# An attention and feed-forward kernel: VectorE copies transposed tiles out ahead of the bias and minimum of the row four ahead

## The chip, the cores and the metric

The kernel runs on one core of a Trainium2 chip. The time is device microseconds of one execution: 1320.96 us, the median of three runs (1320.94 to 1322.1).

## The reference

The input x is 4 batches of 1024 tokens with 128 channels, all float32. Attention has 16 heads of 64 channels; heads are worked two at a time, and such two are called a pair here.

```python
q, k, v = jnp.einsum('bsx,xMnd->Mbnsd', x, qkv)
a = jnp.einsum('bnsd,bntd->bnst', q, k) * 64 ** (-0.5)
cum = jnp.cumsum(rpe_bias, axis=-1)                    # 16 heads x 256 distances
rel = jnp.arange(s)[:, None] - jnp.arange(s)[None, :]
bias = jnp.where(rel >= 0, cum[:, jnp.clip(rel, 0)], -30000.0)   # causal
a = jax.nn.softmax(a + bias, axis=-1)
mix = jnp.einsum('bnst,bntd->bnsd', a, v)
x = layernorm(x + jnp.einsum('bnsd,ndx->bsx', mix, out_w))
# then token-wise: xr, xk mix each token with the one before it
r = sigmoid(xr @ W_r);  k_act = relu(xk @ W_k) ** 2
x = layernorm(x + r * (k_act @ W_v))
```

## The kernel before

**Steps and slots.** The work is 4 batches times 8 pairs of heads, 32 pair steps. A pair step has 16 rows of attention: a row is one head and one tile of 128 queries, and it is as wide as the causal keys before it, 128 x (i + 1) for tile i. `ROWS` lists them: rows 0 to 3 are head 0 with tiles 0 to 3, rows 4 to 7 head 1 with the same tiles, rows 8 to 11 head 0 with tiles 4 to 7, and rows 12 to 15 head 1 with tiles 4 to 7. A step has a slot for each row. Each engine has its own instruction stream, written out by hand in that order of slots, and they meet at counting semaphores.

**A row's way.** TensorE computes the scores into the PSUM tile `ps_rows` (`score`, line 904: q and k are each split into a high and a low part, which are stacked by DMAs). VectorE adds the table of biases and keeps the row's minimum (scores carry the opposite sign), writing to `prob` and `low` (`bias`, line 614). ScalarE takes the exponential and its sum (`exps`, line 470). VectorE takes the reciprocal of the sum (`invert`, line 621). GpSimd multiplies the row by it (`normalise`, line 421). TensorE transposes the row's 128x128 tiles into two PSUM tiles, `ps_t[0]` and `ps_t[1]` in turn (`transpose`, line 918). VectorE or ScalarE copies them to `pt` (`evacuate`, lines 631 and 481): the string `EVACUATOR` names for each of a step's 24 groups of up to four tiles which engine does it. VectorE has those of slots 0, 2, 5, 6, 8 (the first group), 9 (both), 10 (the first), 11 (the first) and 14 (the first). Last, TensorE multiplies `pt` with v into `ps_o` (`mix`, line 934).

**Leads and buffers.** In slot s TensorE, VectorE and ScalarE handle scores, bias and exponential of row s + 4 (`LEAD`), and VectorE the reciprocal of row s + 3; transposes and copies are of row s. `ps_rows` holds four narrow rows or two wide ones: scores of row r wait until VectorE has read the row whose place they take, which is `rows_since(r)` rows earlier: 4 for rows 3 to 7, 3 for rows 1, 2 and 8, 2 for rows 9 to 15 and for row 0. `prob` has eight buffers. A group of transposes waits for the copy of the group two before it.

**The next pair's projections.** In slots 2, 3, 5 and 7 TensorE projects q and k of the next pair (line 879), in slots 10 and 14 v. ScalarE writes the high part (`q_hi`, `k_hi`, line 457) from the PSUM tile `ps_m`, VectorE the remainder (`q_lo`, `k_lo`, line 600), and SyncE's queue then stacks them by DMA. TensorE's next use of `ps_m` waits for the remainder.

**Order within a slot.** TensorE: scores of row s + 4, projection, tile work, `mix` (slots 2, 5 and 11), transposes of row s. ScalarE: high part of the projection, tile work, copies of row s, exponential of row s + 4. VectorE: bias of row s + 4, reciprocal of row s + 3, remainder of the projection, copies of row s, copy of the mixed result to `mix_sb` (slots 6 and 12), tile work. The tile work is output projection, norms and the feed-forward part of one tile of 128 tokens; it is spread over the slots of pair steps 9 to 31. The last batch's eight tiles are worked at the end.

Of the kernel before, what the change touches and what calls it, by code (L numbers as in the profile page):

```python
# [40 lines left out]
def score_at(r):  # L41


    if r < NROWS // 2:
        return BANK * (r % 4)
    width = P * (ROWS[r][1] + 1)
    return SEQ * (r % 2) + ((SEQ - width) // 2 if width - BANK < SHORTEST else 0)
# [41 lines left out]
def build(nc, x, qkv, out_w, rpe, w_r, w_k, w_v, mu_r, mu_k, out):  # L89
# [13 lines left out]
    with ExitStack() as ctx:  # L103
# [148 lines left out]
        def rows_ahead(n, more, slot):  # L252

            if slot + LEAD < NROWS:
                return [(n, slot + LEAD)]
            return [(n + 1, slot + LEAD - NROWS)] if more else []
# [319 lines left out]
        def _(dve):  # L576
# [17 lines left out]
            def project(m, c):  # L594

                dve.wait_ge(s_hi, 4 * m + c + 1)
                which, at = chunk_of(m, c)
                hi, lo, scale = ((q_hi, q_lo, SCALE), (k_hi, k_lo, 1.0))[which]
                half = slice(512 * at, 512 * at + 512)
                nc.vector.scalar_tensor_tensor(out=lo[:, half], in0=proj_bank(m, c), scalar=scale,  # L600
                                               in1=hi[:, half].bitcast(F32), op0=ALU.mult, op1=ALU.subtract)\
                    .then_inc(s_lo, 1)

            def bias(n, r):

                h, i = ROWS[r]
                width = P * (i + 1)
                if i % GROUP == 0:
                    dve.wait_ge(s_table[n % 2][h], 16 * (n // 2) + 16)

                before = (r - PSLOTS) % NROWS
                dve.wait_ge(s_tr, NBANKS * (n if before > r else n + 1) + sum(b[0] <= before for b in BANKS))
                dve.wait_ge(s_score, NROWS * n + r + 1)
                nc.vector.tensor_tensor_reduce(prob[:, r % PSLOTS, 0:width],  # L614
                                               ps_rows[:, score_at(r):score_at(r) + width],
                                               table[n % 2][:, h, SEQ - width:], 1.0, 3.0e38, ALU.add, ALU.min,
                                               low[:, r:r + 1]).then_inc(s_biased, 1)

            def invert(n, r):
                dve.wait_ge(s_exp, NROWS * n + r + 1)  # L620
                nc.vector.reciprocal(inv[:, r:r + 1], total[:, r:r + 1]).then_inc(s_inv, 1)  # L621

            def evacuate(n, k):
                r, b0, nb = BANKS[k]
                h, i = ROWS[r]
                g = i // GROUP
                dve.wait_ge(s_pv, 2 * n + g + 1)
                if n == 0 and r == 2 * GROUP:
                    dve.wait_ge(s_xt_dram, 16)
                dve.wait_ge(s_tr, NBANKS * (n + 1) + k + 1)  # L630
                nc.vector.tensor_copy(pt[h][g][:, b0:b0 + nb, P * (i % GROUP):P * (i % GROUP) + P],  # L631
                                      ps_t[k % 2][:, 0:nb * P].rearrange("p (b s) -> p b s", s=P)).then_inc(s_ev[0], 1)

            def store_mix(n, g):
                dve.wait_ge(s_pv, 2 * n + g + 3)
                dve.wait_ge(s_mix_d[g], 16 * n + 16)
                nc.vector.tensor_copy(mix_sb[g][:, :], ps_o[:, :]).then_inc(s_o, 1)  # L637
# [66 lines left out]

            def step(n, prev, tile_too, more):
                for slot in range(NROWS):
                    for row in rows_ahead(n, more, slot):
                        bias(*row)
                    for row in rows_ahead(n, more, slot - 1):
                        invert(*row)  # L710
                    if more and slot in PROJ_SLOTS[:4]:
                        project(n + 1, PROJ_SLOTS.index(slot))
                    for k in range(NBANKS):
                        if BANKS[k][0] == slot and EVACUATOR[k] == "0":
                            evacuate(n, k)
                    if prev and slot == MIX_FAR[1] + 1:
                        store_mix(n - 1, 1)
                    if slot == MIX_NEAR + 1:
                        store_mix(n, 0)
                    if tile_too:  # L720
                        tile_step(n, slot)

            drive(step)

            def add_residual(w):
# [359 lines left out]
```

## Time and profile before

| | |
|---|---|
| median of three runs | 1320.96 us |
| the profiled execution, its own time | 1322.12 us |
| its span, first to last instruction | 1320.3 us |
| mean granted TensorE clock | 0.965 |
| TensorE, matmuls | 1121.6 us busy, 85% |
| VectorE | 890.1 us busy, 67% |
| ScalarE | 745.8 us busy, 56% |
| GpSimd | 590.8 us busy, 45% |

The profile is of one execution. A busy share is an average over the whole span, a start-up and an end among it. In its views PE is TensorE, DVE is VectorE, ACT ScalarE, POOL GpSimd and SPq the DMA queue of SyncE. A row such as `PE ps_t L918 [0.77 <-DVE pt L631]` says that TensorE stood idle for 0.77 us before the transposes of line 918, and that what ended it was VectorE's copy of line 631. Names of tiles stand without their buffer numbers.

### The profile page before, as it was taken

The numbers are of one execution on the slowest core, as the hardware profiler recorded it, in microseconds if no ns is written. First come the engines' busy times: TensorE is split into PE (matmuls) and PEld (weight loads), VectorE is DVE, ScalarE is ACT, GpSimd is POOL, SyncE is SP. The second block draws the span as 40 slices with busy tenths as digits, with TensorE's granted clock in tenths as the row PEclk, the third lists the DMA queues.
The fourth block names the chain that finished last, engine by engine and source line by source line (L and its number), as shares of the span: only waits on it lengthen the run. The fifth ranks groups of instructions, "written<-read, shape, count | busy, mean of one in ns | idle before, by whom it ended". The sixth has DMA issues, their size and how long they took to land.

```text
span 1320.3 us, 21982 instructions
## 1 busy us (share of the span) xinstructions
PE 1121.6 (85%) x6909; PEld 784.3 (59%) x6909; DVE 890.1 (67%) x2505; ACT 745.8 (56%) x1857; POOL 590.8 (45%) x527
## 2 busy tenths in 40 slices
PE   4424999999999898988998989889898988998985
PEld 2313666666666666666666666656666666666664
DVE  1422666666667777777777777777777787777756
ACT  2312666666665656565566566656656565566532
POOL 1221555555554444454444454544444454444420
PEclk9666999999999999999999999999999999999987
DMA  5775555555555445566544555655555565544610
GB/s 142 167 85 143 130 131 130 130 130 131 140 130 124 116 126 134 126 150 155 127 117 117 133 124 144 150 130 118 132 126 133 128 150 142 120 119 111 205 35 19
DMA packets 104353, 168.38 MB, mean 128 GB/s; under 512 B 10656, under 2 KB 66352, under 8 KB 104240
## 3 DMA queue, kind: packets, MB, share of 16 engines
q1 hardware_dynamic: 104240, 166.98, 52.9%
q8 instruction: 58, 0.95, 0.3%
q14 instruction: 55, 0.45, 0.1%
HBM read 41.63 MB, written 24.64 MB: 50 GB/s over the span
## 4 chain that ended last, share of the span: by engine, by line
PE 61%; DVE 16%; issue 7%; DMA 6%; ACT 6%; SPq 2%; POOL 1%; DVEq 0%; ACTq 0%
PE ps_o L934 20%; PE ps_t L918 15%; PE ps_rows L904 12%; PE ps_m L879 6%; DMA bias_by_distance<-x_t 5%; DVE prob L614 4%; PE ps_m L948 3%; DVE pt L631 3%; PE ps_m L884 3%; DVE shift L681 2%; ACT pt L481 2%; DVE mix_sb L637 2%; DVE k_lo L600 1%; ACT prob L470 1%; DVE q_lo L600 1%
## 5 line engine op out<-in xcount | busy, mean ns | idle before, releaser
L421 POOL TENSOR_TENSOR prob<-prob,inv 128x128 f32<-128x128 f32 (+7 forms) x512 | 583.5, 1147 | 676.8 <-DVE inv L621 676.2
L470 ACT ACTIVATE prob<-prob,low 128x128 f32<-128x128 f32 (+7 forms) x512 | 395.3, 773 | 144.7 <-DVE low L614 140.5
L614 DVE CUSTOM_DVE_ANT_0 prob<-ps_rows,table 128x128 f32<-128x128 f32 (+7 forms) x512 | 383.2, 748 | 120.8 <-PE ps_rows L904 90.4
L904 PE MATMUL ps_rows<-stacks 128*128 128x512 f32 (+3 forms) x1536 | 403.7, 373 | 64.0 <-DMA stacks<-k_lo 40.2
L918 PE MATMUL ps_t<-ident,prob 128*128 128x128 f32 x2304 | 351.8, 280 | 101.1 <-ACT pt L481 64.1
L918 PEld LDWEIGHTS ps_t<-ident,prob 128*128 128x128 f32 x2304 | 262.6, 141 | 213.4 <-issue 123.4
L904 PEld LDWEIGHTS ps_rows<-stacks 128*128 128x128 f32 x1536 | 247.4, 192 | 82.3 <-DMA stacks<-k_lo 40.5
L631 DVE COPY pt<-ps_t 128x256 f32<-128x256 f32 (+2 forms) x320 | 178.5, 566 | 163.5 <-PE ps_t L918 162.4
L481 ACT ACTIVATE pt<-ps_t 128x128 f32<-128x128 f32 (+2 forms) x448 | 203.4, 476 | 146.8 <-PE ps_t L918 146.8
L934 PE MATMUL ps_o<-pt,v_pair 128*64 128x512 f32 (+3 forms) x1536 | 268.7, 492 | 0.0
L934 PEld LDWEIGHTS ps_o<-pt,v_pair 128*64 128x64 f32 x1536 | 101.9, 137 | 181.8 <-issue 172.3
L879 PE MATMUL ps_m<-x_cur,w_cur 128*128 128x512 f32 x250 | 131.9, 610 | 3.9 <-DVE q_lo L600 2.4
L621 DVE RECIPROCAL inv<-total 128x1 f32<-128x1 f32 x512 | 81.7, 160 | 66.0 <-ACT prob L470 64.4
L457 ACT ACTIVATE q_hi<-ps_m 128x512 fp32r<-128x512 f32 x63 | 37.2, 590 | 120.0 <-PE ps_m L879 117.5
L470 ACT ACTIVATION_READ_ACCUMULATOR prob<-prob,low 128x1 f32 x512 | 98.1, 192 | 0.0
L884 PE MATMUL ps_m<-w_cur,x_cur 128*128 128x128 f32 x504 | 66.4, 275 | 0.0
L884 PEld LDWEIGHTS ps_m<-w_cur,x_cur 128*128 128x128 f32 x504 | 65.2, 192 | 0.0
L600 DVE SCALAR_TENSOR_TENSOR q_lo<-ps_m,q_hi 128x512 fp32r<-128x512 f32 x63 | 43.6, 692 | 30.4 <-ACT q_hi L457 30.4
L491 ACT ACTIVATE lnv<-mv,eps 128x1 f32<-128x1 f32 x48 | 14.1, 294 | 80.5 <-DVE mv L683 43.6
L879 PEld LDWEIGHTS ps_m<-x_cur,w_cur 128*128 128x128 f32 x250 | 43.5, 191 | 14.9 <-issue 6.8
L462 ACT ACTIVATE v_pair<-ps_m 128x512 f32<-128x512 f32 x63 | 37.6, 596 | 25.9 <-PE ps_m L884 25.5
L948 PE MATMUL ps_m<-wo,mix_tile 128*128 128x128 f32 x384 | 47.4, 277 | 0.0
(106 smaller groups left out, 607.6 us busy)
## 6 DMA issues: line engine op xcount, KB each, us to landing
stacks<-k_hi SPq DMA_DIRECT2D x124, 256.0 KB, 4.9
stacks<-k_lo SPq DMA_DIRECT2D x124, 256.0 KB, 4.9
stacks<-q_hi SPq DMA_DIRECT2D x62, 256.0 KB, 4.5
stacks<-q_lo SPq DMA_DIRECT2D x62, 256.0 KB, 4.8
mix_transposed<-mix_sb SPq DMA_DIRECT2D x62, 256.0 KB, 2.0
table<-bias_by_distance SPq DMA_DIRECT2D x64, 192.0 KB, 2.6
mix_tile<-mix_transposed SPq DMA_DIRECT2D x24, 512.0 KB, 4.8
w_cur<-in_L_attn_qkv SPq DMA_DIRECT2D x32, 192.0 KB, 3.2
```

The source lines that it names most:

```text
L421: nc.gpsimd.tensor_tensor(row, row, inv[:, r:r + 1].broadcast_to([P, width]), ALU.mult)\
L470: nc.scalar.activation(row, row, ACT.Exp, bias=low[:, r:r + 1], scale=-1.0, accum_out=total[:, r:r + 1]).then_inc(s_exp, 1)
L481: nc.scalar.activation(pt[h][g][:, b0:b0 + nb, P * (i % GROUP):P * (i % GROUP) + P], ps_t[k % 2][:, 0:nb * P].rearrange("p (b s) -> p b s" ...
L614: nc.vector.tensor_tensor_reduce(prob[:, r % PSLOTS, 0:width], ps_rows[:, score_at(r):score_at(r) + width], table[n % 2][:, h, SEQ - width ...
L621: nc.vector.reciprocal(inv[:, r:r + 1], total[:, r:r + 1]).then_inc(s_inv, 1)
L631: nc.vector.tensor_copy(pt[h][g][:, b0:b0 + nb, P * (i % GROUP):P * (i % GROUP) + P], ps_t[k % 2][:, 0:nb * P].rearrange("p (b s) -> p b s ...
L879: ins = nc.tensor.matmul(proj_bank(m, c), w_cur[m % 2][:, which, :], x_cur[:, 512 * at:512 * at + 512], start=True, stop=True)
L884: ins = nc.tensor.matmul(proj_bank(m, c)[:, P * t:P * t + P], x_cur[:, at:at + P], w_cur[m % 2][:, 2, :], start=True, stop=True)
L904: ins = nc.tensor.matmul(ps_rows[:, at + c0:at + c1], q_st(h, n)[:, P * i:P * i + P], k_st(h, n, low_part)[:, c0:c1], start=(low_part == 0 ...
L918: ins = nc.tensor.transpose(ps_t[k % 2][:, P * b:P * b + P], prob[:, r % PSLOTS, at:at + P], ident[:, :])
L934: ins = nc.tensor.matmul(ps_o[D * h:D * h + D, c0:], v_pair[n % 2][:, j, D * h:D * h + D], pt[h][g][:, j, c0:], start=(j == 0), stop=(j == ...
L948: ins = nc.tensor.matmul(ps_m[:, 0:C], mix_tile[:, p, :], wo[:, p, :], start=(p == 0), stop=(p == PAIRS - 1))
```

## The change

VectorE's stream alone is reordered. In each slot the bias and minimum of row s + 4 and the reciprocal of row s + 3 move behind the projection's remainder and the copies of row s. They still stand ahead of the copy to `mix_sb` and of the tile work. The slots without a remainder or a copy of VectorE (1, 4, 12, 13 and 15) stay as they were.

```diff
--- before.py
+++ after.py
@@ -704,15 +704,15 @@
 
             def step(n, prev, tile_too, more):
                 for slot in range(NROWS):
-                    for row in rows_ahead(n, more, slot):
-                        bias(*row)
-                    for row in rows_ahead(n, more, slot - 1):
-                        invert(*row)
                     if more and slot in PROJ_SLOTS[:4]:
                         project(n + 1, PROJ_SLOTS.index(slot))
                     for k in range(NBANKS):
                         if BANKS[k][0] == slot and EVACUATOR[k] == "0":
                             evacuate(n, k)
+                    for row in rows_ahead(n, more, slot):
+                        bias(*row)
+                    for row in rows_ahead(n, more, slot - 1):
+                        invert(*row)
                     if prev and slot == MIX_FAR[1] + 1:
                         store_mix(n - 1, 1)
                     if slot == MIX_NEAR + 1:
```

## Rows read from the trace of the kernel before

**Rows 1.** The page, busy us of each engine (share of the span).

```profile
PE 1121.6 (85%) x6909; PEld 784.3 (59%) x6909; DVE 890.1 (67%) x2505; ACT 745.8 (56%) x1857; POOL 590.8 (45%) x527
```

**Rows 2.** Windows, 300 to 1200 us: busy us (instructions) of each engine, granted clock, DMA share.

```profile
300.00:1200.00 900.00, 815.44 (x5086) 570.29 (x5083) 667.78 (x1864) 549.79 (x1388) 436.00 (x381) 1.00 0.55 132
```

**Rows 3.** Waits, 300 to 1200 us: us in total, times, longest.

```profile
DVE pt L631 <- PE ps_t L918: 121.5, 96, 2.7
...
PE ps_t L918 <- ACT pt L481: 51.4, 47, 1.3
...
PE ps_t L918 <- DVE pt L631: 20.6, 27, 1.2
```

**Rows 4.** Timeline of TensorE, one tile step: start, us, operation, count, idle before.

```profile
710.66 0.55 PE L918 MATMUL ps_t<-ident,prob 128*128 128x128 f32 x3
...
714.14 0.95 PE L904 MATMUL ps_rows<-stacks 128*128 128x512 f32 x4
...
718.18 0.44 PE L918 MATMUL ps_t<-ident,prob 128*128 128x128 f32 x2
...
719.52 1.18 PE L904 MATMUL ps_rows<-stacks 128*128 128x512 f32 x4
...
723.01 0.96 PE L904 MATMUL ps_rows<-stacks 128*128 128x512 f32 x4
...
725.18 0.85 PE L918 MATMUL ps_t<-ident,prob 128*128 128x128 f32 x6 [0.77 <-DVE pt L631]
...
735.21 0.85 PE L918 MATMUL ps_t<-ident,prob 128*128 128x128 f32 x6 [0.96 <-ACT pt L481]
```

**Rows 5.** Timeline of VectorE, the same step.

```profile
711.31 0.56 DVE L631 COPY pt<-ps_t 128x384 f32<-128x384 f32 x1 [2.34 <-PE ps_t L918]
...
718.72 0.42 DVE L631 COPY pt<-ps_t 128x256 f32<-128x256 f32 x1 [0.63 <-PE ps_t L918]
...
724.35 0.69 DVE L631 COPY pt<-ps_t 128x512 f32<-128x512 f32 x1
...
732.43 0.69 DVE L631 COPY pt<-ps_t 128x512 f32<-128x512 f32 x1 [1.41 <-PE ps_t L918]
```

**Rows 6.** Groups by shape, 300 to 1200 us: count, busy us, mean ns, idle before.

```profile
L614 DVE CUSTOM_DVE_ANT_0 prob<-ps_rows,table 128x1024 f32<-128x1024 f32 x48 | 58.2, 1213 | 1.9 <-PE ps_rows L904 1.8
...
L614 DVE CUSTOM_DVE_ANT_0 prob<-ps_rows,table 128x896 f32<-128x896 f32 x48 | 52.1, 1086 | 10.7 <-PE ps_rows L904 10.6
...
L470 ACT ACTIVATE prob<-prob,low 128x896 f32<-128x896 f32 x48 | 50.0, 1042 | 57.6 <-DVE low L614 55.8
...
L614 DVE CUSTOM_DVE_ANT_0 prob<-ps_rows,table 128x768 f32<-128x768 f32 x48 | 45.5, 949 | 0.0
...
L614 DVE CUSTOM_DVE_ANT_0 prob<-ps_rows,table 128x512 f32<-128x512 f32 x48 | 33.1, 689 | 3.5
...
L600 DVE SCALAR_TENSOR_TENSOR q_lo<-ps_m,q_hi 128x512 fp32r<-128x512 f32 x47 | 32.5, 692 | 17.5 <-ACT q_hi L457 17.5
...
L470 ACT ACTIVATE prob<-prob,low 128x384 f32<-128x384 f32 x47 | 28.6, 608 | 0.0
...
L457 ACT ACTIVATE q_hi<-ps_m 128x512 fp32r<-128x512 f32 x47 | 27.7, 590 | 90.2 <-PE ps_m L879 90.2
...
L614 DVE CUSTOM_DVE_ANT_0 prob<-ps_rows,table 128x384 f32<-128x384 f32 x47 | 25.5, 542 | 2.3 <-PE ps_rows L904 2.3
```

**Rows 7.** Timeline of TensorE, one step without tile work.

```profile
266.77 0.55 PE L918 MATMUL ps_t<-ident,prob 128*128 128x128 f32 x3
...
269.53 0.94 PE L904 MATMUL ps_rows<-stacks 128*128 128x512 f32 x4
...
280.58 0.85 PE L918 MATMUL ps_t<-ident,prob 128*128 128x128 f32 x6 [1.21 <-DVE pt L631]
```

**Rows 8.** Timeline of ScalarE, the tile step of rows 4.

```profile
733.35 1.14 ACT L470 ACTIVATE prob<-prob,low 128x1024 f32<-128x1024 f32 x1
```

**Rows 9.** Timeline of TensorE, after slot 11 of the first step.

```profile
115.20 0.80 PE L904 MATMUL ps_rows<-stacks 128*128 128x256 f32 x2 [40.24 <-DMA stacks<-k_lo]
```

## The prediction

> **What bounds the kernel now.** I read the page's head first: of a span of 1320.3 us TensorE is busy for 85% of it, VectorE (DVE) for 67%, ScalarE (ACT) for 56% [rows 1]. The stretch from 300 to 1200 us, which the loop of pair steps fills, has TensorE busy for 815 of 900 us at granted clock 1.00, its 2.4 GHz level [rows 2]. So TensorE sets the pace, and a change elsewhere counts only where it moves one of TensorE's waits. Next the table of waits for that stretch: TensorE waits before its transposes 51.4 us for ACT's copies of transposed tiles and 20.6 us for DVE's, while DVE spends 121.5 us waiting for the transposes it is to copy [rows 3]. The last number is the one to keep in mind: on DVE the copy is an instruction that often waits for TensorE, and what stands behind it waits too. Last the timelines of a pair step, one engine at a time, to see which wait ends last in each slot [rows 4, 5, 8].
>
> **What the change moves.** Nothing is added or removed: 16 slots per pair step, and in each DVE ran bias(s+4), invert(s+3), then projection remainder and copies of slot s. Now the remainder and the copies come first. DVE copies in slots 0, 2, 5, 6, 8, 9 (two), 10, 11, 14: there the bias of row s+4, which needed only scores that TensorE computes at the slot's start, now waits for the transposes that TensorE makes at the slot's end. Three kinds of work wait for that bias: the scores two rows on, since in the wide half two rows fill the PSUM area (row 9 needs bias 7, row 11 needs bias 9, row 13 needs bias 11); ACT's exponential, and behind it in ACT's queue the next projection copy (q_hi, k_hi) and ACT's own copies of transposes; and DVE's q_lo or k_lo, which needs that q_hi or k_hi, with the following bias behind it. The last makes a ladder that crosses from DVE to ACT and back.
>
> The arithmetic: one DVE operation starts some 0.09 us before the printed end of a copy or remainder; a row minimum is readable by ACT about its printed duration after the bias's start, plus 0.03; and from DVE's last result to a matmul I take 0.14, as where the transposes at 725.18 follow the copy that ends at 724.35 + 0.69 = 725.04 [rows 4, 5].
>
> **Place A, scores of row 9 (slot 5).** The transposes of slot 2 follow a long product and end at 710.66 + 0.55 = 711.21; the copy starts at 711.31 [rows 4, 5]. Now behind it: copy 0.47, bias 6 0.54, handover 0.03, its exponential 0.61 on ACT, then q_hi 0.59 (it stood ready before), handover 0.03, q_lo 0.61, bias 7 0.69, handover 0.14 [rows 6]. 711.31 + 3.71 = 715.02, where row 9's scores started at 714.14 [rows 4]: 0.88 us. In a step without the token-wise tile work (the first nine) the copy starts 0.10 after 267.32, and 267.42 + 3.71 = 271.13 against 269.53 [rows 7]: 1.60 us.
>
> **Place B, scores of row 11 (slot 7).** The copy of slot 5 starts at 718.72 and takes 0.33 [rows 5], bias 9 takes 0.95 [rows 6], handover 0.14: 720.14 against 719.52 [rows 4], 0.62 us. It counts from the transposes of slot 5, so it adds to A.
>
> **Place C, scores of row 13 (slot 9).** From the minimum of row 9: copy of slot 6 0.47, bias 10 1.09, 0.03, exponential 10 1.04, k_hi 0.59, 0.03, k_lo 0.61, bias 11 1.21, 0.14 = 5.21. The scores of row 11 start 0.14 after that minimum, and 3.49 us lay between them and those of row 13 before (723.01 - 719.52) [rows 4, 6]. 5.21 - 0.14 - 3.49 = 1.58 us. The copy of the mixed result in slot 6 stands beside ACT's exponential and costs nothing; without that cover it would be at most 0.60.
>
> **What is gained.** The copy of slot 8 no longer stands behind bias 12, and TensorE's wait of 0.77 us for it in slot 9 goes (1.21 in the short step) [rows 4, 7]: after C it would come 0.5 us before TensorE asks. Its sum over the stretch is most of the 20.6 us of [rows 3].
>
> **Place D, transposes of slot 13.** They waited 0.96 us for an ACT copy that stands behind exponential 15 [rows 4]. That began at 733.35 behind ACT's copy of slot 11 [rows 8]. Now bias 15 stands behind DVE's copy of slot 11: 732.43 + 0.60 + 1.21 + 0.03 = 734.27 [rows 5, 6]: 0.92 us later, and all of it reaches TensorE, which waited already. The next wait of that kind (slot 14, through DVE's second normalisation and ACT's reciprocal root) hangs on the same exponential and shifts along, without a term of its own.
>
> Slots 0, 9, 10 and 14: their biases come late too, but TensorE has 16 products in slot 0 and the mixes in slots 2 and 11 before it needs them; I take 0, bounds -0.1 and 0.3 each. GpSimd's normalisation waits for DVE often and is done a slot or more ahead; 0. On SP's queue the stacking of k for the next pair waits for k_lo 3, which comes as late as C has it, and so do the scores that need it: 0; if its slack is gone, up to 1 us a step. A lies between 0 (if q_hi gets ahead) and 1.60, C between 0.3 (no ladder through ACT) and 2.2 (with the copy of the mix in it).
>
> **Sum.** A tile step: 0.88 + 0.62 + 1.58 - 0.77 + 0.92 = 3.23; a short one 1.60 + 0.62 + 1.58 - 1.21 + 0.92 = 3.51. There are 22 tile steps with a next pair and 8 short ones after the first. In the first step the delay falls into the 40.24 us for which TensorE waits for a DMA anyway [rows 9]: 0. The last has no projection, hence no ladder: 1, from B, D and the lost wait. 22 x 3.23 + 8 x 3.51 + 1 = 100 us. The profiled execution took 1322.1 us with a span of 1320.3, and the runs' median is 1321.0: 1421 us on the runs' scale.
>
> A rule that speaks for this: the Trainium skill (PSUM — Partial Sum Buffer, Engine vs sequencer instructions) has DVE's, ACT's and GpSimd's queues as strict FIFO. By it a ready bias can't pass a waiting copy, and the sum is the 100 us above; were it not so, A to D would be near nothing and the 27 us of gain (rival 1) would stand. No row before the change has a ready bias behind a waiting copy for long, so the trace leaves it to the result.
>
> **Rivals.** (1) *Slack takes it up: faster.* Rows are scored four ahead and the probabilities have eight buffers; DVE idles a third. If the bias of row s+4 were back before TensorE reaches the scores two rows on, only the gain is left: 22 x 0.77 + 8 x 1.21 = 27 us, 1294 us. It decides at B: 0.90 us lie between the end of slot 5's transposes and row 11's scores, and the way over DVE takes 1.52. Against it is that every term of B is a row. (2) *Direct waits only.* The ladders through ACT are shorter than I put them, because waits that I count as new overlap: B and D remain, less the gain: (0.77 x 22 + 0.33 x 8) = 20 us, 1341 us. For it: ACT is busy only 56% [rows 1]. (3) *Knock-on.* The late biases use up SP's slack and the stacks of the next pair arrive late, 1 us a step more: 1451 us. (4) *The clock falls.* More short waits let TensorE's granted clock drop from its 2.4 to its 1.2 GHz level. For a tenth of the 815 us in which it is busy that would be some 80 us more: 1500 us. Against it: the clock stays at 1.00 through waits of 0.77 and 0.96 us in every step [rows 2, 4]. The Trainium skill (TensorE: Matmul & The Clock Gate, A second HAM failure mode) warns of such cycling through PSUM with short idles; the trace so far does not show it.
>
> **Chances.** Forecast 0.62; rival 1 0.06; rival 2 0.16; rival 3 0.11; rival 4 0.03; 0.02 that nothing measurable happens. A difference under about 0.2% can't be told from none. Faster 0.06, same 0.03, slower 0.91. The forecast's own range is 1390 to 1440 us; to leave out no more than two in ten I take 1350 to 1450.
>
> **What would show it.** Right: bias rows directly behind copies on DVE; a new entry "TensorE scores wait for DVE's row minimum" of some 3 us a step, at rows 9, 11 and 13; "ACT exponential waits for DVE" much larger; TensorE's wait for DVE's copies near nothing; the wait in slot 13 near 1.9 us; a tile step of 41.3 us. Wrong: no wait before the scores of row 11 (B fails and with it all), or waits at B and D alone (rival 2), or scores of row 0 that wait for a stack DMA (rival 3), or a clock below 1.00 (rival 4).

## The result

The changed kernel took 1450.36 us (median of four runs, 1448.45 to 1452.84), the kernel before 1321.53 in the same set: a ratio of 1.0969, 95% interval 1.0954 to 1.0984. It is 129 us slower, where 100 were forecast. Among all runs below, two executions ran in a slower state, one of copies_only (1465.8 us, mean clock 0.901) and one of the kernel before (2828 us), and no ratio uses them.

The page of the changed kernel, busy us of each engine, and the window of 300 to 1200 us (busy us and instructions, granted clock, DMA share, GB/s), beside [rows 1, 2]:

```profile
PE 1178.6 (81%) x6909; PEld 808.7 (56%) x6909; DVE 879.4 (61%) x2505; ACT 750.2 (52%) x1857; POOL 594.2 (41%) x527
```

```profile
300.00:1200.00 900.00, 772.90 (x4566) 529.98 (x4566) 586.51 (x1669) 497.37 (x1253) 397.09 (x346) 0.98 0.49 119
```

The instructions are the same and in the same number. TensorE issued 5086 of its matmuls in this stretch before, 4566 now. Its busy sum over the whole span has grown by 57 us for the same 6909 matmuls, and the granted clock has left 1.00: some matmuls ran at the lower level. That isn't all of the 57 us: all_but_slot11 below keeps the clock at 1.00 in this stretch and has 1152.2 us, 31 more than before. The profile models the ends of matmuls, so the sum of their times is a rough measure of TensorE's work.

Its waits from 300 to 1200 us (us in total, times, longest), beside [rows 3]; the first line is of the kernel before, the others of the changed one:

```profile
ACT prob L470 <- DVE low L614: 86.6, 93, 3.0
```

```profile
ACT prob L470 <- DVE low L614: 308.1, 208, 4.5
DVE pt L631 <- PE ps_t L918: 217.1, 143, 3.5
...
PE ps_t L918 <- POOL prob L421: 42.3, 22, 1.9
...
PE ps_rows L904 <- DVE low L614: 35.3, 63, 1.3
...
PE ps_t L918 <- ACT pt L481: 23.0, 39, 1.6
...
PE ps_m L879 <- DVE y L650: 4.5, 19, 0.6
...
PE ps_t L918 <- DVE pt L631: 1.8, 7, 0.4
```

TensorE's wait for DVE's copies has gone from 20.6 to 1.8 us: the copies do come earlier. DVE spends 217 instead of 121.5 us in front of copies, and ACT's exponentials wait 308 instead of 87 us for DVE. A new line stands there: the scores wait 63 times, three times a step, for a row minimum. It sums to 35.3 us, some 1.7 us a step, where the prediction looked for some 3: the scores come nearly as late as forecast, but part of the lateness shows on other lines (TensorE waits 0.80 us for q_lo at 783.14 before it transposes x1, 0.39 before) or between other instructions. The entry "POOL prob" is slot 13's wait under another name: GpSimd's release is the last one the profile can pair with it, but row 13 had been normalised at 759.22 + 1.47 = 760.69 us, 4.6 us before the transposes began. What came last is ACT's copy, which begins at 764.53 and frees the first of its two PSUM tiles at about 765.1.

TensorE's timeline in the changed kernel, slots 13 and 14 of one tile step and 2 to 9 of the next, beside [rows 4]:

```profile
765.25 1.01 PE L918 MATMUL ps_t<-ident,prob 128*128 128x128 f32 x6 [1.92 <-POOL prob L421]
...
766.71 1.91 PE L884 MATMUL ps_m<-w_cur,x_cur 128*128 128x128 f32 x8
...
779.45 0.55 PE L918 MATMUL ps_t<-ident,prob 128*128 128x128 f32 x3
...
783.75 0.98 PE L904 MATMUL ps_rows<-stacks 128*128 128x512 f32 x4 [0.17 <-DVE low L614]
784.85 1.10 PE L879 MATMUL ps_m<-x_cur,w_cur 128*128 128x512 f32 x2
...
788.18 0.44 PE L918 MATMUL ps_t<-ident,prob 128*128 128x128 f32 x2
...
790.08 1.20 PE L904 MATMUL ps_rows<-stacks 128*128 128x512 f32 x4 [0.31 <-DVE low L614]
...
795.13 0.98 PE L904 MATMUL ps_rows<-stacks 128*128 128x512 f32 x4 [1.05 <-DVE low L614]
...
796.39 0.82 PE L918 MATMUL ps_t<-ident,prob 128*128 128x128 f32 x6
```

And DVE's and ACT's, beside [rows 5, 8]: the copy of slot 11 with bias 15 behind it, then the one of slot 5 with bias 9; and exponential 15.

```profile
761.52 0.69 DVE L631 COPY pt<-ps_t 128x512 f32<-128x512 f32 x1 [2.38 <-PE ps_t L918]
762.13 1.22 DVE L614 CUSTOM_DVE_ANT_0 prob<-ps_rows,table 128x1024 f32<-128x1024 f32 x1
...
788.73 0.42 DVE L631 COPY pt<-ps_t 128x256 f32<-128x256 f32 x1 [1.42 <-PE ps_t L918]
789.07 0.95 DVE L614 CUSTOM_DVE_ANT_0 prob<-ps_rows,table 128x768 f32<-128x768 f32 x1
```

```profile
763.39 1.15 ACT L470 ACTIVATE prob<-prob,low 128x1024 f32<-128x1024 f32 x1 [0.84 <-DVE low L614]
```

Before, bias 15 ran in the time in which DVE now stands idle for 2.38 us before slot 11's copy. Measured from the start of the long product of slot 2 to the next, a tile step went from 38.10 to 42.07 us, a step without tile work from 34.40 to 38.09. These are the usual lengths; some steps are up to 1.8 us longer, and the experiments show why.

### The profile page after: what moved, and what is told of

Read it like the earlier page. It is cut to its first block, busy times and chain, and to the rows that moved or that the text cites. A ratio compares the mean times of both kernels' runs of the same rounds, so it can differ in the third digit from the quotient of the medians.

```text
span 1451.1 us, 21982 instructions
## 1 busy us (share of the span) xinstructions
PE 1178.6 (81%) x6909; PEld 808.7 (56%) x6909; DVE 879.4 (61%) x2505; ACT 750.2 (52%) x1857; POOL 594.2 (41%) x527
## 4 chain that ended last, share of the span: by engine, by line
PE 59%; DVE 15%; issue 12%; ACT 6%; DMA 6%; SPq 1%; POOL 1%; DVEq 0%; ACTq 0%
PE ps_o L934 18%; PE ps_t L918 14%; PE ps_rows L904 13%; DVE prob L614 7%; PE ps_m L879 6%; DMA bias_by_distance<-x_t 5%; PE ps_m L948 3%; PE ps_m L884 3%; ACT prob L470 2%; DVE shift L681 2%; DVE pt L631 1%; ACT pt L481 1%; POOL prob L421 1%; ACT q_hi L457 1%; PE ps_rows L1007 1%
## 5 line engine op out<-in xcount | busy, mean ns | idle before, releaser
L904 PE MATMUL ps_rows<-stacks 128*128 128x512 f32 (+3 forms) x1536 | 412.5, 378 | 118.5 <-DVE low L614 80.0
L918 PE MATMUL ps_t<-ident,prob 128*128 128x128 f32 x2304 | 367.9, 286 | 104.2 <-POOL prob L421 60.2
L918 PEld LDWEIGHTS ps_t<-ident,prob 128*128 128x128 f32 x2304 | 273.0, 145 | 217.0 <-POOL prob L421 111.4
L904 PEld LDWEIGHTS ps_rows<-stacks 128*128 128x128 f32 x1536 | 251.2, 194 | 158.4 <-DVE low L614 80.2
L884 PE MATMUL ps_m<-w_cur,x_cur 128*128 128x128 f32 x504 | 78.6, 307 | 0.0
L884 PEld LDWEIGHTS ps_m<-w_cur,x_cur 128*128 128x128 f32 x504 | 74.0, 218 | 4.0 <-issue 4.0
L600 DVE SCALAR_TENSOR_TENSOR k_lo<-ps_m,k_hi 128x512 fp32r<-128x512 f32 x62 | 42.9, 691 | 45.8 <-ACT k_hi L457 45.8
L948 PEld LDWEIGHTS ps_m<-wo,mix_tile 128*128 128x128 f32 x384 | 46.1, 196 | 0.0
L637 DVE COPY mix_sb<-ps_o 128x512 f32<-128x512 f32 x64 | 43.6, 681 | 2.0 <-PE ps_o L934 2.0
```

The source lines that it names most:

```text
L884: ins = nc.tensor.matmul(proj_bank(m, c)[:, P * t:P * t + P], x_cur[:, at:at + P], w_cur[m % 2][:, 2, :], start=True, stop=True)
L904: ins = nc.tensor.matmul(ps_rows[:, at + c0:at + c1], q_st(h, n)[:, P * i:P * i + P], k_st(h, n, low_part)[:, c0:c1], start=(low_part == 0 ...
L918: ins = nc.tensor.transpose(ps_t[k % 2][:, P * b:P * b + P], prob[:, r % PSLOTS, at:at + P], ident[:, :])
L948: ins = nc.tensor.matmul(ps_m[:, 0:C], mix_tile[:, p, :], wo[:, p, :], start=(p == 0), stop=(p == PAIRS - 1))
```

## The experiments

All of them rearrange DVE's slot as in this diff; `EARLY` names the slots with the new order (the changed kernel has all sixteen).

```diff
+                    rows() if slot not in EARLY else None      # bias(s+4), invert(s+3)
+                    remainder()                                # project(n + 1, ...)
+                    copies()                                   # evacuate(n, k) of this slot
+                    rows() if slot in EARLY else None
```

Step lengths in us, a step without tile work and a tile step, read from TensorE's timelines as above; where some were longer, the length without a fall of the clock first:

| kernel | no tile work | tile step | median us |
|---|---|---|---|
| before | 34.40 | 38.10 | 1321.5 |
| changed | 38.09 | 42.07 | 1450.4 |
| slots2and3_alone | 35.96 | 39.32 | 1361.4 |
| slot5_alone | 34.94 | 38.63 | 1338.5 |
| slots5to8 | 35.39 | 39.40 | 1358.4 |
| slot11_alone | 35.35, 36.95 | 39.30, 40.97 | 1385.6 |
| slot11_filled | 35.35 | 39.30 | 1362.7 |
| all_but_slot11 | 37.18 | 40.88 | 1406.5 |
| changed_filled | 38.10 | 42.07 | 1442.3 |
| slot8_alone | 33.70 | 37.87 | 1310.9 |
| slot8_and_late_exp | 33.70 | 37.43 | 1301.6 |

### Place A: slots 2 and 3

```diff
+EARLY = (2, 3)
```

> The new order in slots 2 and 3 alone (place A). Theory: the scores of row 9 start 0.88 us later in a tile step and 1.6 in one without; 22 x 0.88 + 8 x 1.6 = 32 us, 1353 us. The changed kernel shows in addition 0.3 us between these scores and the next projection, because ScalarE's copy of the transposed x1 stands behind exponential 7; if that belongs to this place, 39 us, 1360 us. Rival, DVE makes it up by slot 9 where TensorE waits anyway: at most 0.77 us a step given back, 1336 us.

Measured: 1361.41 us, ratio 1.0295 (1.0280 to 1.0310), 40 us more. Steps are 1.56 us longer without tile work (1.60 forecast) and 1.22 with it (0.88 forecast). In a tile step the scores of row 9 themselves come 0.81 us late, counted from the start of slot 2's transposes (736.64 - 732.35 = 4.29 us here, 3.48 before). Another 0.33 stands right behind them: 737.75 - 736.64 = 1.11 us lie between these scores and the third projection, where 0.78 lay before (784.85 - 783.75 = 1.10 in the changed kernel). ACT's copy of the transposed x1, which frees `ps_m`, stands behind exponential 7. Nothing is made up later: the wait in slot 9 is still 0.77 us.

### Place B: slot 5

```diff
+EARLY = (5,)
```

> The new order in slot 5 alone (place B). Theory of the prediction, each place costs its own term: the scores of row 11 start 0.56 to 0.62 us later, 31 x 0.6 = 19 us, 1340 us. Rival, the terms don't add but share a cover: what sets the transposes of slot 9 before is a chain through bias 10, which moves by only 0.43 us, and the wait of 0.77 us there shrinks by the rest: 31 x 0.43 = 13 us, 1334 us.

Measured: 1338.52 us, ratio 1.0121 (1.0106 to 1.0136), 16 us more, 0.54 us a step. The time lies between the two theories' 0.43 and 0.6; the timeline decides. The rival needs the wait in slot 9 to shrink by 0.2 us, and it has not:

```profile
1082.04 0.85 PE L929 MATMUL ps_t<-ident,prob 128*128 128x128 f32 x6 [0.76 <-DVE pt L632]
```

It was 0.77 us before. All of place B reaches the end of the step.

### Places B and C and the lost wait: slots 5 to 8

```diff
+EARLY = (5, 6, 7, 8)
```

> The new order in slots 5 to 8: place B, place C and the lost wait of slot 9 together, without A and D. Theory, the places add up: the changed kernel's step is 3.97 us longer, of which A alone took 1.22 and D alone 1.20 in a tile step, so 1.55 remain; in a step without tile work 3.70 - 1.56 - 0.95 = 1.19. 23 x 1.55 + 8 x 1.19 = 45 us, 1367 us, the clock at its upper level. Rival, places share their cover (A's delay is part of C's): over 2 us a step here, 1385 us.

Measured: 1358.35 us, ratio 1.0270 (1.0248 to 1.0293). Steps grew by 0.99 and 1.30 us, so places C and slot 8 together cost 0.45 and 0.76 us; 1.58 - 1.21 = 0.37 and 1.58 - 0.77 = 0.81 were forecast. The expectation took all that A and D left for this group and was 0.2 us a step too high. The places are nearly independent: 1.56 + 0.99 + 0.95 = 3.50 of 3.69 us, and 1.22 + 1.30 + 1.20 = 3.72 of 3.97. Of the rest, some 0.2 us a tile step stand in slot 0, where the copy now delays the bias and with it the first addition of the tile work, for which the projection waits (the line "DVE y L650" above). Without tile work some 0.2 us come from slot 14: in all_but_slot11 the exponential of row 2 waits 0.39 us for its bias, which now stands behind slot 14's copy, ACT's copies of slot 15 follow that exponential, and TensorE waits for them 0.39 us before the transposes of slot 0, where it waited 0.16.

### Place D: slot 11, and the clock

```diff
+EARLY = (11,)
```

> The new order in slot 11 alone. Theory of place D: exponential 15 starts 0.92 us later and ScalarE's copies for slot 13 with it, so TensorE's wait in slot 13 is 1.9 us instead of 0.96: 31 x 0.92 = 29 us more, 1350 us, with the clock at its upper level throughout. Rival, that the long wait also brings the clock down as it stood at 0.50 in the changed kernel after it: 0.3 to 0.5 us more in each of the 23 tile steps, 1357 to 1362 us, and a granted clock below 1.00 in slots 13 and 14 of the tile steps.

Measured: 1385.61 us, ratio 1.0484 (1.0419 to 1.0549), 63 us more: twice what the place was worth by the first theory, and beyond the second too. TensorE's timeline of slots 13 to 15 in a long tile step:

```profile
728.24 0.85 PE L929 MATMUL ps_t<-ident,prob 128*128 128x128 f32 x6 [1.91 <-POOL prob L422]
...
729.28 1.82 PE L895 MATMUL ps_m<-w_cur,x_cur 128*128 128x128 f32 x8
731.91 1.73 PE L929 MATMUL ps_t<-ident,prob 128*128 128x128 f32 x7 [0.81 <-ACT pt L482]
...
734.29 1.91 PE L929 MATMUL ps_t<-ident,prob 128*128 128x128 f32 x8
```

The wait is 1.91 us, as place D said. But behind it the seven transposes take 1.73 us instead of 0.96 and the v projection 1.82 instead of 1.05: TensorE is at its 1.2 GHz level here, with a granted clock of 0.50 from 730 to 736 us. To see whether the wait is the cause, the next kernel fills it, with the scores of row 1 computed five times over instead of once:

```diff
-                    for low_part in range(2):
+                    for low_part in (0, 1) * (5 if r == 1 and n > 0 else 1):
```

> The new order in slot 11 alone, as before, and TensorE computes the scores of row 1 five times over (the same numbers, in the 0.5 us each that fall into slot 13's wait of 1.9 us): more work, in a wait. Theory, the time beyond place D's 29 us is the clock, which falls after that wait: with the wait filled to some 0.6 us it stays up, 1351 to 1357 us, faster than without the added work (1386 us). Rival, the clock is not tied to this wait, or the late exponential costs more than D says: 1386 us or above.

Measured: 1362.67 us, ratio 1.0312 (1.0271 to 1.0353). TensorE does 248 matmuls more than in slot11_alone and the kernel is 23 us faster. The same slots in its timeline:

```profile
712.45 1.43 PE L915 MATMUL ps_rows<-stacks 128*128 128x256 f32 x10
714.86 0.84 PE L929 MATMUL ps_t<-ident,prob 128*128 128x128 f32 x6 [0.97 <-POOL prob L422]
715.46 0.60 PE L915 MATMUL ps_rows<-stacks 128*128 128x384 f32 x2
715.90 1.05 PE L895 MATMUL ps_m<-w_cur,x_cur 128*128 128x128 f32 x8
718.53 0.96 PE L929 MATMUL ps_t<-ident,prob 128*128 128x128 f32 x7 [1.58 <-ACT pt L482]
```

The wait is cut to 0.97 us, the clock stays up, and all but a few steps are 35.35 or 39.30 us long. So place D by itself is 0.95 us without tile work, as forecast, and 1.20 with it. The 0.25 more in a tile step is in slot 14's wait, 1.58 us here against 1.33 in the kernel before:

```profile
738.63 0.95 PE L918 MATMUL ps_t<-ident,prob 128*128 128x128 f32 x7 [1.33 <-ACT pt L481]
```

It goes with DVE's second addition of the tile work (the last section). The time came out 6 to 12 us above the expectation; four of its tile steps were still 40.9 us long.

> The changed kernel with the old order in slot 11. Theory D: the wait in slot 13 is back at 0.96 us. If D counts 0.95 to 1.2 us a step and nothing else goes, 31 x 1.0 = 31 us less than the changed kernel, 1419 us. If the low stretches of the clock come from slot 13's wait of 1.9 us alone, they go too, and another 5 to 30 us with them, 1389 to 1414 us, with steps all of one length and a granted clock of 1.00 from 400 us on.

```diff
+EARLY = tuple(s for s in range(16) if s != 11)
```

Measured: 1406.45 us, ratio 1.0641 (1.0625 to 1.0657), 44 us less than the changed kernel, within the second theory. 8 x 0.91 + 23 x 1.19 = 35 of them are the steps of usual length; the other 9 should then be the clock's. The changed kernel with slot 13's wait filled in the same way tests that:

```diff
+EARLY = tuple(range(16))
-                    for low_part in range(2):
+                    for low_part in (0, 1) * (5 if r == 1 and n > 0 else 1):
```

> The changed kernel, with the scores of row 1 computed five times over in slot 13's wait of 1.9 us. Removing slot 11's part from the changed kernel gave 44 us, of which 8 x 0.91 + 23 x 1.19 = 35 us are the steps of full clock; theory: the remaining 9 us are the clock's, and with the wait filled they go, 1441 us, all tile steps 42.07 us long. Rival: other waits of the changed kernel, 1.05 us before the scores of row 13 the longest, keep the clock falling, 1450 us.

Measured: 1442.27 us, ratio 1.0916 (1.0893 to 1.0940), 8 us less than without the added work, and the window of 300 to 1300 us is at 1.00 again:

```profile
300.00:1300.00 1000.00, 869.88 (x5303) 597.17 (x5302) 668.65 (x1871) 554.30 (x1398) 443.15 (x386) 1.00 0.49 119
```

For comparison the changed kernel, where the clock falls after slot 13's wait for some 3 us (columns: busy us and instructions of PE, PEld, DVE, ACT, POOL, then the granted clock):

```profile
761.60:764.00 2.40, 1.69 (x14) 1.32 (x12) 2.40 (x5) 1.21 (x2) 0.49 (x1) 1.00 0.77 165
764.00:766.00 2.00, 0.75 (x7) 0.78 (x7) 1.74 (x7) 1.66 (x6) 2.00 (x2) 0.95 0.77 225
766.00:768.00 2.00, 2.00 (x11) 2.00 (x10) 1.93 (x4) 0.23 (x1) 1.04 (x1) 0.50 0.38 136
768.00:770.00 2.00, 1.69 (x11) 1.43 (x11) 0.79 (x5) 1.97 (x7) 0.40 (x1) 0.70 0.11 33
```

### Copies alone, remainder alone

```diff
-                    remainder()
                     copies()
                     rows()
+                    remainder()
```

> In all slots only the copies move ahead of bias and reciprocal; the projection's remainder stays behind them, in the order copies, bias, reciprocal, remainder. Theory: places B (0.54) and D (0.95) and the gain of slot 8 are the copies' own and stay; place C goes, because bias 11 no longer waits for k_lo, and place A shrinks from a late bias 7 to a late q_lo before the transpose of x1, up to 0.7 us in tile steps. Sum 0.8 to 1.4 us a step and the clock's part of slot 11 (30 us), 1375 to 1400 us. Rival, the copies are harmless and the remainder does it all: within 10 us of 1322.

Measured: 1442.9 us, ratio 1.0907 (1.0885 to 1.0928). Both theories fail: the copies alone cost nearly as much as the whole change. Place C did shrink: row 13's scores start 717.53 - 713.17 = 4.36 us after row 11's, against 5.05 in the changed kernel and 3.49 before (from [rows 4]). What I had missed is in slot 3, TensorE's timeline and then DVE's:

```profile
704.34 1.17 PE L889 MATMUL ps_m<-x_cur,w_cur 128*128 128x512 f32 x2 [1.39 <-DVE q_lo L601]
```

```profile
702.60 0.56 DVE L632 COPY pt<-ps_t 128x384 f32<-128x384 f32 x1 [4.61 <-PE ps_t L928]
...
703.62 0.67 DVE L601 SCALAR_TENSOR_TENSOR q_lo<-ps_m,q_hi 128x512 fp32r<-128x512 f32 x1
```

The remainder q_lo of slot 2 now stands behind that slot's copy, which waits for the transposes behind the long product, and TensorE can't project again before it. In the old order and in the changed one the remainder is ahead of that copy. The timelines are of the execution of 1465.8 us. They show the order that makes the wait; how long it is in the other executions wasn't seen, and how the 121 us divide over the places wasn't measured.

```diff
                     remainder()
-                    copies()
                     rows()
+                    copies()
```

> In all slots only the projection's remainder moves ahead of bias and reciprocal (slots 2, 3, 5 and 7), the copies stay behind. Theory: bias 7 waits for q_lo, the scores of row 9 0.5 us late; bias 11 waits for k_lo, the scores of row 13 1.4 us late and the transposes of slot 9 some 0.7 us, as they waited already. About 1.2 us a step, 31 x 1.2 = 37 us, 1359 us, clock at its upper level. Rival, the copies do it all: within 5 us of 1322.

Measured: 1404.33 us, ratio 1.0634 (1.0611 to 1.0656), 83 us more where 37 were expected. TensorE's timeline of a tile step has part of place A, most of place C and, since slot 8's copy still stands behind bias 12, the old wait after it:

```profile
716.31 0.96 PE L914 MATMUL ps_rows<-stacks 128*128 128x512 f32 x4 [0.16 <-DVE low L615]
717.42 1.10 PE L889 MATMUL ps_m<-x_cur,w_cur 128*128 128x512 f32 x2
...
722.11 1.18 PE L914 MATMUL ps_rows<-stacks 128*128 128x512 f32 x4
...
726.84 0.97 PE L914 MATMUL ps_rows<-stacks 128*128 128x512 f32 x4 [1.05 <-DVE low L615]
...
729.01 0.85 PE L928 MATMUL ps_t<-ident,prob 128*128 128x128 f32 x6 [0.76 <-DVE pt L632]
```

Row 13's scores start 726.84 - 722.11 = 4.73 us after row 11's, 1.24 later than before (1.56 in the changed kernel). The scores of row 9 are 0.42 late, counted from the start of the long product, and the third projection another 0.33, as in place A. Together with 0.09 between them these are the 2.08 us by which a tile step is longer. I had expected some 0.7 us of it to come out of the wait in slot 9; bias 12 and the copy are late by as much as the scores, so nothing does. The usual steps are 36.8 and 40.2 us. About every second one of those without tile work is 1.5 us longer, and of the tile steps every second one from 750 us on is 1.6 us longer, while eight in a row before that are not; the mean clock is 0.954. So the two halves cost 121 and 83 us and the whole 129: they don't add. For the copies alone the q_lo wait above, which neither other order has, is part of the reason; the rest of the overlap wasn't taken apart. In the long steps the same two waits stand, and behind them the clock falls:

```profile
766.99 0.97 PE L914 MATMUL ps_rows<-stacks 128*128 128x512 f32 x4 [1.05 <-DVE low L615]
...
769.16 1.46 PE L928 MATMUL ps_t<-ident,prob 128*128 128x128 f32 x6 [0.76 <-DVE pt L632]
...
770.28 1.84 PE L914 MATMUL ps_rows<-stacks 128*128 128x512 f32 x4
```

The six transposes take 1.46 us instead of 0.85 and row 14's scores 1.84 instead of 1.06; the window of 768 to 772 us has a granted clock of 0.66, the one of 728 to 732 us has 1.00. No wait here is as long as place D's, but two stand 2.2 us apart. The two waits can't be all of it: the eight tile steps before have them too and stay at 1.00. Whether their sum matters was not tried, and why some steps fall and others don't is left open.

### What pays: slot 8

```diff
+EARLY = (8,)
```

> The new order in slot 8 alone, the old one in the other fifteen. My theory: this is the part of the change that pays. TensorE's wait of 0.77 us (1.21 in a step without tile work) before the transposes of slot 9 goes, and bias 12, 0.6 us later, reaches the scores of row 14 in time: 23 x 0.7 + 8 x 1.1 = 25 us less than before, some 1296 us. Rival (a ready bias must never stand behind a copy): bias 12 late holds the scores of row 14 for as long as the wait that went, no gain, 1321 us or a little more.

Measured: 1310.9 us, ratio 0.9915 (0.9900 to 0.9930), 11 us faster, where 25 were expected. It gains 0.70 us a step without tile work and 0.23 with it. In a step without tile work the wait in slot 9 has shrunk from 1.21 to 0.39 us:

```profile
276.77 0.85 PE L929 MATMUL ps_t<-ident,prob 128*128 128x128 f32 x6 [0.39 <-DVE pt L632]
```

In a tile step it is gone, and another has come, in slot 10:

```profile
716.78 0.85 PE L929 MATMUL ps_t<-ident,prob 128*128 128x128 f32 x6
...
718.81 1.13 PE L895 MATMUL ps_m<-w_cur,x_cur 128*128 128x128 f32 x8 [0.30 <-ACT xk_t L504]
```

The rectifier copy that frees `ps_m` stands on ACT behind exponential 12. That one is not needed before slot 12, so it can stand behind:

```diff
+                    if slot == 9:
+                        exps(n, 12)                 # ScalarE, behind the tile work
...
+                    if slot != 8:
                         for row in rows_ahead(n, more, slot):
                             exps(*row)
```

> The new order in slot 8 alone, and on ScalarE the exponential of row 12 behind the tile work of slot 9 instead of ahead of it. In slot8_alone bias 12 comes 0.6 us later, ScalarE's exponential 12 with it, and behind that the rectifier copy of the tile work, for which TensorE's v projection of slot 10 waited 0.30 us; the gain in a tile step was 0.23 of 0.77 us. Theory: that wait goes, 23 x 0.3 = 7 us less than slot8_alone's 1311, 1304 us. Rival, the wait for bias 12 before the scores of row 14 takes its place: 1311 us.

Measured: 1301.64 us, ratio 0.9849 (0.9835 to 0.9862), 9 us less than slot8_alone, faster than both kernels. 1304 were expected. The v projection doesn't wait, and a tile step is 37.43 us long:

```profile
713.32 0.85 PE L932 MATMUL ps_t<-ident,prob 128*128 128x128 f32 x6
...
714.89 1.05 PE L898 MATMUL ps_m<-w_cur,x_cur 128*128 128x128 f32 x8
```

## Why the prediction was right, and what it mis-sized

The direction, the mechanism and all four places were right; the size was 29 us short. The measured 1450.4 us lies 0.4 us beyond the range's upper end of 1450; the ratio on the 1320.96 us from which the forecast was made gives 1449.0, just inside it, so the range held only barely. The forecast's own 1390 to 1440 was missed. The time alone would speak for rival 3 with its 1451 us, whose mechanism isn't there. In the order of the prediction:

- **Copies that wait, and biases behind them.** Shown by the timelines of slots 5 and 11, and place by place by the kernels that change a slot alone. The rule from the Trainium skill (PSUM — Partial Sum Buffer, Engine vs sequencer instructions), that DVE's queue is strict FIFO, is borne out: bias 15, whose scores were there, stood behind a copy that waited 2.38 us.
- **Place A**: 1.60 forecast and 1.56 measured without tile work; 0.88 and 1.22 in a tile step. Of the 0.88 for the scores 0.81 came; the term left out ACT's copy of x1 behind exponential 7, 0.33.
- **Place B**: 0.62 and 0.54.
- **Place C less the gain of slot 8**: 0.37 and 0.45; 0.81 and 0.76. In the timeline 5.05 us lie between the two scores where the forecast had 5.07. The step "it would come 0.5 us before TensorE asks" held: in the changed kernel the copy ends at 795.07 + 0.67 = 795.74 us and the transposes begin at 796.39, without a wait. Where slot 8 is changed without C, the copy is not always in time: 0.39 us of wait stay in a step without tile work.
- **Place D**: 0.92 and 0.95; in a tile step 1.20. "Shifts along, without a term of its own" failed there by 0.25 us.
- **Slots with 0**: slot 0 costs some 0.2 us a tile step and slot 14 some 0.2 us a step without tile work, both within the bound given, by the timelines. Neither was changed alone, nor were slots 9 and 10; what is left for those after the other places is under 0.1 us a step.
- **The sum**: 3.23 a tile step against 3.97, 3.51 against 3.69. 22 x 0.74 + 8 x 0.18 = 18 of the 29 us missing. Of the other 11, 8 are **the clock** by changed_filled; 3 are not accounted for. I had the clock as a rival with a chance of 0.03, because waits of 0.77 and 0.96 us had left it at 1.00 (those of 1.21 and 1.33 us in the same kernel did too), and then priced place D with a wait of 1.9 us without asking whether that holds for such a wait. The rival was not the likeliest case, but it was no separate case either: it comes with place D. A clock below 1.00 was named as a sign against the forecast, and it came (0.98 in the window).
- **Rival 1** (faster by the lost wait alone) is false for the whole, but slot 8 alone is just that, at 11 instead of 27 us. **Rival 2** (direct waits only): false, all of A and C is there. **Rival 3** (late stacks): no such line in the table of waits.

## What to carry to other kernels

An instruction that waits belongs behind all that is ready in its queue, unless something critical waits for it: ask of each pair, not of each kind, since slot 8 gained here while slots 2 and 3, 5 and 11 lost. When a hand-written order is changed at several places, add up the waits place by place along the engine that sets the pace; then see how long each wait gets in all, since a long one may bring TensorE's clock down and cost again behind it. When a wait goes, look for what stands next behind the instruction that you delayed: here a second, smaller move took the gain from 11 to 20 us.

## What the runs showed of the hardware

- **A wait under 2 us can bring TensorE's clock down, and work of no use can keep it up.** After waits of 1.9 us in slot 13 the next 3 to 7 us ran at the 1.2 GHz level in many steps, not in all; with the wait cut to 0.97 us nearly never. Filling it made slot11_alone 23 us and the changed kernel 8 us faster. The longest wait isn't the whole rule: in remainder_only, with none above 1.33 us from 300 to 1200 us, the clock still fell in some steps, while slots5to8, which has the same 1.05 us before the scores of row 13, kept it at 1.00. The Trainium skill (TensorE: Matmul & The Clock Gate, A second HAM failure mode) tells of a kernel whose clock cycles because TensorE idles shortly and often between groups of matmuls. These traces agree that short idles can do it, but waits of 0.77, 0.96 and 1.33 us in every tile step of the kernel before left it at 1.00.
- **DVE's operations with two SBUF inputs ended 0.14 to 0.15 us after the GpSimd operation beside them.** DVE in the kernel before and in the changed one, at slot 12's second addition:

```profile
735.62 1.28 DVE L681 TENSOR_TENSOR shift<-y,x 128x128 f32<-128x128 f32 x1
```

```profile
765.66 1.52 DVE L681 TENSOR_TENSOR shift<-y,x 128x128 f32<-128x128 f32 x1
```

GpSimd in the changed kernel:

```profile
756.92 1.36 POOL L421 TENSOR_TENSOR prob<-prob,inv 128x640 f32<-128x640 f32 x1 [0.37 <-DVE inv L621]
...
763.51 3.53 POOL L421 TENSOR_TENSOR prob<-prob,inv 128x896 f32<-128x896 f32 x2 [2.82 <-DVE inv L621]
```

The addition ends at 767.18, GpSimd's two rows at 767.04; in the kernel before at 736.90, and GpSimd's row at 736.75; in slot11_filled at 716.79 and 716.65. The product just ahead of it, of the same shape but with one input in PSUM, took 0.28 us beside the same GpSimd row (at 735.30 in the kernel before). The square of the tile work (line 672, the same shape) took 0.27 us at 756.76, just before GpSimd began, and 1.15 us in the kernel before, beside GpSimd. So a late bias, which puts GpSimd's rows 14 and 15 back to back, makes DVE's tile work 0.24 us longer: the 0.25 us of place D. That this is the cause was not tried by itself. The Trainium skill (SBUF — State Buffer, Who interferes with whom) has the second of two SBUF inputs of a DVE instruction come through a read interface shared with GpSimd, which is an exclusive lock; that fits.
